# A macaron block on one core: the next input loaded into the right-side buffer and normalised before the group ends

## The reference

```
x = x + 0.5 * gated_ffn(layernorm(x))          # 256 -> 768 -> 256, integer weights
x = x + gated_delta_attention(layernorm(x))    # 16 heads, key 64, value 128, conv of 4 taps
x = x + 0.5 * gated_ffn(layernorm(x))
x = x + 0.5 * token_shift_ffn(layernorm(x))
x = x + block_attention(layernorm(x))          # 16 heads of 16, blocks of 64
x = x + 0.5 * token_shift_ffn(layernorm(x))
```

## Time and profile before

| what | value |
|---|---|
| median of three executions | 8609.14 us |
| the profiled execution's own time | 8607.54 us |
| its span, first to last instruction | 8605.7 us |
| mean granted clock of TensorE in it | 0.894 of full speed |
| TensorE busy (matmuls) | 81% |
| VectorE busy | 54% |
| ScalarE, GpSimd busy | 30%, 26% |

### The profile page before, as it was taken

The page is one execution under the profiler, slowest core; times in us unless marked ns, Lnnn a source line. Parts: engine busy times, 40 slices in busy tenths (PEclk is TensorE's granted clock), DMA queues, the critical chain, the costliest instruction groups (busy, mean ns, idle before and its releaser), DMA issues. The chain is left out here.

```text
span 8605.7 us, 157131 instructions
## 1 busy us (share of the span) xinstructions
PE 6932.5 (81%) x57416; PEld 4998.7 (58%) x57416; DVE 4672.9 (54%) x10083; ACT 2623.3 (30%) x5274; POOL 2271.0 (26%) x3553
## 2 busy tenths in 40 slices
PE   7788887877878788887888878788787888878886
PEld 4665646556565565656656466565655656556564
DVE  6446464554645546565464645546455464554643
ACT  3223242332423214232242422324232142322421
POOL 1403223041321413314132230423304133141321
PEclk9888988898988888988889888889888999888997
DMA  1100101001000100001000010010000100010000
GB/s 50 33 23 20 39 14 31 26 20 44 19 20 25 28 36 19 21 29 25 33 19 25 28 31 26 19 44 19 20 26 24 39 19 20 29 25 35 19 22 3
DMA packets 376003, 225.76 MB, mean 26 GB/s; under 512 B 336880, under 2 KB 353392, under 8 KB 366960
## 3 DMA queue, kind: packets, MB, share of 16 engines
q1 hardware_dynamic: 375152, 214.71, 8.4%
HBM read 155.95 MB, written 58.72 MB: 25 GB/s over the span
## 5 line engine op out<-in xcount | busy, mean ns | idle before, releaser
L773 DVE SCALAR_TENSOR_TENSOR PS<-SC,CW,PS 128x512 f32<-128x512 f32 x1536 | 1156.3, 754 | 167.6 <-DVEq L771 75.7
L1478 PE MATMUL PS<-CST,SC 128*128 128x128 f32 x2776 | 480.6, 314 | 560.1 <-PEq L1531 258.6
L1475 PE MATMUL PS<-S,KQ 64*64 64x128 f32 x8192 | 769.2, 309 | 0.0
L1478 PEld LDWEIGHTS PS<-CST,SC 128*128 128x128 f32 x2776 | 353.8, 159 | 698.6 <-issue 680.4
L986 POOL TENSOR_TENSOR RSTD<-VAR,NHALF 128x2 f32<-128x2 f32 x200 | 143.0, 715 | 2322.9 <-POOLq L985 2177.6
L1145 POOL TENSOR_TENSOR FR<-MS,NHALF 128x8 f32<-128x8 f32 x128 | 210.1, 1641 | 1501.3 <-POOLq L1144 1298.4
L1475 PEld LDWEIGHTS PS<-S,KQ 64*64 64x64 f32 x8192 | 562.3, 156 | 73.1 <-issue 72.4
L1475 PE MATMUL PS<-XT,WV 128*128 128x512 f32 x1024 | 548.7, 665 | 58.5 <-PEq L1776 58.5
L1475 PE MATMUL PS<-XT,WQK 128*128 128x512 f32 x1024 | 559.9, 685 | 0.0
L1475 PE MATMUL PS<-SC 128*64 128x32 f32 (+1 forms) x2720 | 333.0, 334 | 264.5 <-PEq L1600 151.5
L1069 POOL TENSOR_TENSOR WO<-WO 128x30 f32<-128x30 f32 (+14 forms) x960 | 507.3, 528 | 136.4
(11 more groups left out here) (156 smaller groups left out, 12756.0 us busy)
## 6 DMA issues: line engine op xcount, KB each, us to landing
WV<-in_wv SPq DMA_DIRECT2D x16, 2048.0 KB, 11.7
WO<-in_wo SPq DMA_DIRECT2D x16, 2048.0 KB, 7.8
WQK<-in_wq SPq DMA_DIRECT2D x16, 1024.0 KB, 5.2
WQK<-in_wk SPq DMA_DIRECT2D x16, 1024.0 KB, 7.3
cells_in<-SC SPq DMA_DIRECT2D x128, 128.0 KB, 2.7
WO<-cells_in SPq DMA_DIRECT2D x32, 512.0 KB, 3.3
cells_out<-WO SPq DMA_DIRECT2D x32, 512.0 KB, 2.6
cells_nat<-WO SPq DMA_DIRECT2D x32, 512.0 KB, 3.6
```

Source lines behind the costliest of these rows:

```text
L773: op = v.scalar_tensor_tensor(y, pre[:, j:j + G], CW[:, i * TAPS + j:i * TAPS + j + 1], y, ALU.mult, ALU.add)
L1475: return nc.tensor.matmul(out_, l, r, start=start, stop=stop)
L1478: return nc.tensor.matmul(out_, in_, ident, is_transpose=True, start=True, stop=True)
```

## The change

The next x is no longer loaded into XS. It goes into R, as soon as DVE has taken the mean square of chunk 6 (`r_free`). DVE takes its statistics between `mean_square(7)` and `normalise(7)`, normalises it into XN between `normalise(7)` and `projected(3)`, and the down stage of the first feed-forward reads x from R and writes the sum to XS, once SP has seen the stores landed (`xs_free`). As x then lies over the first quarter of WV, the value weights are loaded only when DVE has made that sum (`x_used`), and TensorE waits for them at value tile 0 (`wv_back`). The input of the first group is normalised ahead of the loops. After the last group the first rows of x are loaded and normalised once more, and nothing uses them. POOL's two `rstd` of the new input move from the head of a group to the end of the one before.

```diff
@@ SP
-            def load(row, p):
-                sp.dma_start(v3(XS[p], NT), x_in[bass.ds(row, G), :].rearrange("(t p) d -> p t d", p=P)).then_inc(x_loaded, 16)
+            def load(row):
+                sp.dma_start(v3(R, NT), x_in[bass.ds(row, G), :].rearrange("(t p) d -> p t d", p=P)).then_inc(x_loaded, 16)
...
-            def load_qkv():
-                for dst, src in ((WQ, wq), (WK, wk), (WV[:, :], wv)):
+            def load_qk():
+                for dst, src in ((WQ, wq), (WK, wk)):
                     sp.dma_start(dst, src).then_inc(qkv_back, 16)
+
+            def load_v():
+                sp.wait_ge(x_used, 1)
+                sp.sem_inc(x_used, -1)
+                sp.dma_start(WV[:, :], wv).then_inc(wv_back, 16)
...
+            def next_x(row):
+                sp.wait_ge(r_free, 1)
+                sp.sem_inc(r_free, -1)
+                load(row)
+
+            def next_qk():
                 sp.wait_ge(chunks_done, 1)
                 sp.sem_inc(chunks_done, -1)
-                load_qkv()
+                load_qk()
...
             with sp.Fori(0, B * GROUPS // 2 - 1) as n:
                 for p in range(2):
+                    load_v()
                     inverse_traffic()
+                    next_x(n * (2 * G) + (p + 2) * G)
                     store(n * (2 * G) + p * G, p)
-                    load(n * (2 * G) + (p + 2) * G, p)
-                    next_qkv()
+                    sp.sem_inc(xs_free, 1)
+                    next_qk()
@@ DVE
+            def input_stats():
+                dve.wait_ge(x_loaded, 16)
+                dve.sem_inc(x_loaded, -16)
+                stats(0, R)
+                stats(1, R)
+
+            def input_normal():
+                normal(0, R, XN, xn_ready)
+                normal(1, R, XN, xn_ready)
+
             def first_ffn(x):
-                stats(0, x)
-                stats(1, x)
-                normal(0, x, XN, xn_ready)
-                normal(1, x, XN, xn_ready)
                 xt_copy()
...
-                    v.scalar_tensor_tensor(x[:, cols], bank(6 + k), 0.25 * W_SCALE ** 3, x[:, cols], ALU.mult, ALU.add)
+                    if k == 0:
+                        dve.wait_ge(xs_free, 1)
+                        dve.sem_inc(xs_free, -1)
+                    i = v.scalar_tensor_tensor(x[:, cols], bank(6 + k), 0.25 * W_SCALE ** 3, R[:, cols], ALU.mult, ALU.add)
+                    if k == 1:
+                        i.then_inc(x_used, 1)
...
                     if c >= 1:
                         mean_square(c - 1)
+                    if c == CHUNKS - 1:
+                        dve.drain().then_inc(r_free, 1)
                     fill(FILL[c][2])
...
                 mean_square(CHUNKS - 1)
-                fill(FILL[CHUNKS][1])
+                input_stats()
                 normalise(CHUNKS - 1, 0)
                 normalise(CHUNKS - 1, 1)
-                fill(FILL[CHUNKS][2])
+                input_normal()
                 projected(NT - 1, XS[p])
...
             dve.drain()
+            input_stats()
+            input_normal()
             with dve.Fori(0, B) as b:
...
                 for p in range(2):
-                    dve.wait_ge(x_loaded, 16)
-                    dve.sem_inc(x_loaded, -16)
                     first_ffn(XS[p])
@@ POOL
+                rstd(0)
+                rstd(1)
...
             with pool.Fori(0, B * GROUPS) as n:
-                for k in (0, 1, 0, 1):
+                for k in (0, 1):
                     rstd(k)
@@ TensorE
+                    if i == QK_TILES:
+                        pe.wait_ge(wv_back, 16)
+                        pe.sem_inc(wv_back, -16)
...
-                pe.wait_ge(qkv_back, 48)
-                pe.sem_inc(qkv_back, -48)
+                pe.wait_ge(qkv_back, 32)
+                pe.sem_inc(qkv_back, -32)
```

More of the change, by code:

```diff
@@ L201, in bass_macaron @@
         x_loaded = sem("x_loaded")
+        x_used = sem("x_used")
+        xs_free = sem("xs_free")
+        r_free = sem("r_free")
+        wv_back = sem("wv_back")
         x_final = sem("x_final")
@@ L415, in inverse_traffic @@
                 sp.dma_start(WO[:, :], wo).then_inc(wo_back, 16)
-            def next_qkv():
+            def next_x(row):
[3 more added lines that the diff above has]
+            def next_qk():
                 sp.wait_ge(chunks_done, 1)
                 sp.sem_inc(chunks_done, -1)
-                load_qkv()
+                load_qk()
             sp.wait_ge(w_cleared, 1)
-            load(0, 0)
-            load_qkv()
+            load(0)
+            load_qk()
+            sp.sem_inc(xs_free, 1)
+            load_v()
             inverse_traffic()
+            next_x(G)
             sp.wait_ge(x_final, 2)
             sp.sem_inc(x_final, -2)
-            load(G, 1)
-            next_qkv()
+            sp.sem_inc(xs_free, 1)
+            next_qk()
             with sp.Fori(0, B * GROUPS // 2 - 1) as n:
                 for p in range(2):
+                    load_v()
                     inverse_traffic()
+                    next_x(n * (2 * G) + (p + 2) * G)
                     store(n * (2 * G) + p * G, p)
-                    load(n * (2 * G) + (p + 2) * G, p)
-                    next_qkv()
+                    sp.sem_inc(xs_free, 1)
+                    next_qk()
+            load_v()
             inverse_traffic()
+            next_x(0)
             store((B * GROUPS - 2) * G, 0)
```

## The result

| | before | changed |
|---|---|---|
| median of four executions | 8609.06 us | 8546.90 us |
| lowest to highest | 8606.76 to 8609.47 us | 8542.07 to 8565.03 us |
| profiled execution (its span) | 8607.54 (8605.7) us | 8542.67 (8540.9) us |
| mean granted clock | 0.894 | 0.901 |

The ratio is 0.9932, with a 95% interval of 0.9919 to 0.9944. The change saves 62 us where 23 were forecast, and the range ended at 8558. The sign was right, the size was 2.7 times too small.

A forecast was written before the change was run, and what follows sets the result against it. TensorE, busy 81%, was taken as the bound, with 3.3 us more at the start of every p=0 group. Sum: 8609.14 - 23.5 (seven p=0 groups) + 0.4 (first group) = 8586.0 us; range 8558 to 8608.

The forecast's parts named there:

- The part removed: Group's head: x wait, statistics, powers, normalisation go; 0 at 8 p=1 groups, 3.35 us at each of 7 p=0 groups.
- p=1 groups: Groups starting behind the first half of a sequence, 522.3 us before; the branch hides the chain, so gain 0.
- p=0 groups: Groups starting behind the second half of a sequence, 525.6 us before; seven later ones forecast to gain 3.35 us each.
- The value weights: Load moved from group's end to after the first feed-forward's sum; 43 us of slack before value tile 0, cost 0.
- The faster branch: Rival at TensorE's loop branch: quiet queues without WV save 1 us for each of 15, 8571 us; chance 0.16.
- The paid delay: Rival before `normalise(7)`: statistics' 0.8 us paid in all 16 groups, 12.8 us, 8599 us; forecast took 0; chance 0.20.
- the equal 510.7 us: Stretch from the clock's rise to the group's branch, equal in both kinds of group; taken to show small start differences vanish.
- late clock: Rival at the output projection: longer TensorE pause delays the clock's rise, 3.35 us per group, +30 us, 8639 us; chance 0.12.
- Transfers: SP's load of x: issued at 1573.4, landing at 1577.5, 7 us before DVE asks at 1584.6.
- The test that I named: Signs at TensorE's branches: right if all intervals are near 522.3 us, wrong if any group length is neither known one.

The follow-up runs named there:

- wv_late_only: Kernel before, with only the value weights loaded later, behind the down sums of the first feed-forward; 8560.5 us, ratio 0.9942.

## Why the prediction was wrong, step by step

**The part removed.** Right in its mechanism: the branch hides the chain in front of p=1 groups and DVE's own branch exposes it in front of p=0 groups. The size, "7 x 3.35 = 23.5 us", was too small: those seven groups lost 47.7 us. I had capped their gain at the length of a p=1 group, and that length itself fell: the eight p=1 groups, where I had put the gain at 0, lost 20.5 us. With the early normalisation and traffic at the branch none of the eight got shorter, and with the value weights moved alone four of them did.

**The value weights.** This is the step that failed: "43 us of slack, cost 0". The slack was there, and the cost at the new place is 0. But the gain at the old place stood in the sum with nothing, and was left to a rival. With the load gone from there, the instruction packet starts 1 us sooner, TensorE's branch falls by 1.2 us and the idle time at DVE's by 1.65. The load moved alone gives 49 us, shown by one run, and traffic put back makes the branch 5.1 us and brings back 25 us, shown by another.

**The faster branch.** The rival had the mechanism and priced it at 1 us per branch, close to the 1.2 measured, but its time, 8571 us, was too long as well. What was wrong is that a branch was multiplied into the time at its own size, or was thought to be swallowed. A group moved by a step of 3.4 us or not at all. The sentence "small differences of the start are gone by the end" rested on two cases, 510.70 and 510.68 us from the clock's rise to the branch, which is too few: with a start 1.3 us earlier behind the branch that stretch was 507.7 us. By which of the many changes of the clock in a group the 3.0 us come stays open; the missing low stretch in the query and key tiles isn't needed for a group of 518.8 us and doesn't suffice for one.

**The paid delay.** I took 0 for the 0.8 us, and that was right. The runs with less and with more show a plateau: -0.8, 0 and +1.2 us against the change give 8550.7, 8546.9 and 8546.7 us. They don't show that my reason, the equal 510.7 us, was the cause. Behind it comes the rival "late clock" with 70 us for 2.3 us of delay; I had given its whole cost as 53.6 us, and its place and mechanism were as described.

**Transfers.** x landed 3.6 to 4.6 us after its issue and 6 us before it was asked for; right. The first group was forecast 0.4 us later and ended 2.3 later, and behind the last branch, where I had put nothing, it took 1.2 us more. The cause of both is open; the first needs no early normalisation, since wv_late_only's first group ended 2.6 us later.

**The test that I named.** What was to make the prediction wrong was "any group length that isn't one of the two that I know". 518.8 us is such a length.

The Trainium skill (Runtime: NRT & Kernel Launch, Instruction fetch mechanics) says that a taken branch to a page that isn't loaded waits for a DMA fetch. The traces agree: a packet of instructions starts within each taken branch, and the branch took 3.3 us with no data moving, 4.5 us beside the load of the value weights and 5.1 us beside the copy. The 108 ns that the Trainium skill (Advanced Engine Details and Errata, Control Flow Timing) gives a compare-and-branch, which I had set aside, fits none of them; the 79 ns of the branch that leaves the loop come nearer.

## What to carry to other kernels

A load that hides perfectly can still cost: ask what else is fetched at that time, the instructions behind a loop's branch first, and move large loads away from the branches. Where an engine's idle time is followed by a stretch of low clock, a change of 1 us may be worth nothing or several us instead of 1, so scan the delay with a few variants instead of adding up terms. And when the next input is ready before a loop's end, the branch is what is left: write two or four groups into the loop.

## What the runs showed that I hadn't expected

- Group lengths come in steps. In the profiled executions of all kernels whose TensorE loop spans one group, every interval is 518.8, 522.2 or 525.7 us to 0.1, whatever was changed; pairs are 1030.8, 1034.2, 1037.7 or 1044.5 us.
- A delay of 2.3 us in each of 16 groups cost 70 us, and one of 1.2 us nothing.
- 2 MB copied from device memory to device memory, for which no engine waits, lengthened a loop's branch from 3.3 to 5.1 us. Its packet of instructions started 2.3 to 3.0 us into the branch instead of 0.9 to 1.0.
